# Who multiplies the spread values: VectorE or GpSimd, in the lead-in of a two-layer graph convolution

## What the reference computes

```python
def _ngcf_conv(x, W1, W2, src, dst, n_nodes):
    ones = jnp.ones(src.shape[0], dtype=x.dtype)
    deg_out = jnp.clip(jax.ops.segment_sum(ones, src, num_segments=n_nodes), 1.0)
    deg_in = jnp.clip(jax.ops.segment_sum(ones, dst, num_segments=n_nodes), 1.0)
    norm = jax.lax.rsqrt(deg_out[src] * deg_in[dst])
    h_src, h_dst = x[src], x[dst]
    msg = (h_src @ W1 + h_src * h_dst @ W2) * norm[:, None]
    return x @ W1 + jax.ops.segment_sum(msg, dst, num_segments=n_nodes)
h = jax.nn.relu(_ngcf_conv(x, W1_1, W2_1, src, dst, n))
h = _ngcf_conv(h, W1_2, W2_2, src, dst, n)
out = _layernorm(x + h)
```

## Time and profile before

| | us |
|---|---|
| median of 3 runs | 1270.73 (1262.32 to 1270.86) |
| the profiled execution | 1268.42, of it 1266.8 from the first to the last instruction |
| PE busy | 806.7 |
| DVE busy | 1003.4 |
| ACT busy | 715.0 |
| POOL busy | 810.5 |

### The profile page before, as it was taken

One profiled execution on the slowest core, in us unless ns is written; L12 is line 12 of the kernel. 1 busy time (PEld: TensorE's weight loads), 2 busy tenths in 40 slices (PEclk: granted clock), 3 DMA queues, 4 the chain that ended last, 5 costly groups with the idle time before them and its releaser, 6 DMA issues. The chain is left out here.

```text
span 1266.8 us, 33156 instructions
## 1 busy us (share of the span) xinstructions
PE 806.7 (64%) x12938; PEld 743.5 (59%) x12938; DVE 1003.4 (79%) x2582; ACT 715.0 (56%) x2723; POOL 810.5 (64%) x819
## 2 busy tenths in 40 slices
PE   1655367676767677766773566666766666766664
PEld 1554256566666666655662566666666665766664
DVE  8998578888898889888962678778878877788774
ACT  3000046665666566666662266667677667667665
POOL 6000677777777777777734777777777777667600
PEclk9999989988988898899885786888778788887885
DMA  6976112222222222222212133333333333333322
GB/s 130 199 220 280 42 37 52 53 52 52 52 52 52 53 52 52 57 51 58 53 40 58 27 68 68 77 76 76 69 69 76 77 77 77 67 67 80 67 45 48
DMA packets 148617, 93.63 MB, mean 74 GB/s; under 512 B 115880, under 2 KB 128616, under 8 KB 147948
## 3 DMA queue, kind: packets, MB, share of 16 engines
q1 hardware_dynamic: 122872, 64.77, 19.2%
q0 software_dynamic: 25472, 26.34, 12.0%
q10 hardware_dynamic: 116, 0.40, 0.1%
HBM read 52.75 MB, written 38.69 MB: 72 GB/s over the span
## 5 line engine op out<-in xcount | busy, mean ns | idle before, releaser
L591 POOL DMA_INDIRECT c_rows<-table,k_row_i x796 | 789.7, 992 | 395.7 <-issue 237.6
L608 PE MATMUL c_sum<-c_rest,c_sel 128*128 128x64 bf16 x3110 | 388.4, 215 | 0.0
L608 PE MATMUL c_sum<-c_lo,c_sel 128*128 128x64 bf16 x3110 | 388.2, 215 | 0.1
L608 PE MATMUL c_sum<-c_rows,c_sel 128*128 128x64 bf16 x1555 | 213.6, 224 | 201.5 <-DVE c_lo L746 181.9
L608 PEld LDWEIGHTS c_sum<-c_lo,c_sel 128*128 128x128 bf16 x3110 | 337.2, 113 | 0.2 <-issue 0.2
L608 PEld LDWEIGHTS c_sum<-c_rest,c_sel 128*128 128x128 bf16 x3110 | 336.6, 113 | 0.1
L608 PEld LDWEIGHTS c_sum<-c_rows,c_sel 128*128 128x128 bf16 x1555 | 180.2, 119 | 214.1 <-issue 214.1
L608 PE MATMUL c_sum<-c_yr,c_sel 128*128 128x64 bf16 x1555 | 174.1, 206 | 145.7 <-DVE c_lo L746 133.1
L608 PEld LDWEIGHTS c_sum<-c_yr,c_sel 128*128 128x128 bf16 x1555 | 156.9, 107 | 161.8 <-issue 161.8
L731 DVE TENSOR_SCALAR c_sel<-k_place,k_grid 128x512 bf16<-128x512 f16 (+2 forms) x796 | 234.8, 366 | 0.0
L660 ACT ACTIVATE c_sum<-c_sum,k_xh 128x64 f32<-128x64 f32 x784 | 172.1, 348 | 72.2 <-DVE c_sum L762 72.2
(11 more groups left out here) (134 smaller groups left out, 1074.8 us busy)
## 6 DMA issues: line engine op xcount, KB each, us to landing
c_rows<-table,k_row_i POOLq DMA_INDIRECT x796
table<-c_y SPq DMA_DIRECT2D x48, 256.0 KB
c_res<-in_x SPq DMA_DIRECT2D x48, 256.0 KB, 2.9
out<-c_y SPq DMA_DIRECT2D x48, 256.0 KB, 2.6
table<-k_xh SPq DMA_DIRECT2D x2, 3640.0 KB, 10.7
table<-k_xh SPq DMA_DIRECT2D x1, 3542.5 KB, 12.9
table<-k_xh SPq DMA_DIRECT2D x1, 1040.0 KB, 7.0
table<-k_xh SPq DMA_DIRECT2D x1, 520.0 KB, 5.5
```

Source lines behind the costliest of these rows:

```text
L591: nc.gpsimd.indirect_dma_start(out=rows[:, b % RING, i], out_offset=None, in_=tables[l], in_offset=bass.IndirectOffsetOnAxis(ap=k.row_i[:, ...
L608: last = nc.tensor.matmul(p_sum[g % BANKS][:, t - GROUP[g][0], :], sel[:, b % 2, i, n * P:(n + 1) * P], part, start=first and q == 0, stop ...
```

## The change

Frame 0 stays on VectorE. For frames 1 to 8 the four products of `spread` are issued by GpSimd, from the same operands. VectorE makes the two one-hots of a frame one frame earlier than before, so `near_s` and `near_n` have two buffers each. A new semaphore, `near_made`, tells GpSimd that they are there; before it writes, GpSimd also waits until the last piece of frame f-2 is placed. VectorE waits, before it writes a `near` buffer again, until GpSimd has used it (`spread_made`, f-1). TensorE's waits and all of VectorE's other work stay as they were.

```diff
-        near_s, near_n = sb("near_s", [P, WIN, EB * FRAME_PS[0]], F16), sb("near_n", [P, WIN, EB * FRAME_PS[0]], F16)
+        near_s, near_n = ([sb(f"{n}{j}", [P, WIN, EB * FRAME_PS[0]], F16) for j in range(2)] for n in ("near_s", "near_n"))
...
+        def spread_out(engine, f):
+            w = FRAME_PS[f]
+            shape = [P, WIN, EB, w]
+            for a in range(4):
+                last = engine.tensor_tensor(blocks(spread[f % 2][:, a], w), blocks((near_s, near_n)[a == 3][f % 2], w),
+                                            by_raw(value_t[a], f).unsqueeze(1).to_broadcast(shape), ALU.mult)
+            last.then_inc(spread_made, 1)
...
+            pool.wait_ge(copied, 5)
+            for f in range(1, FRAMES):
+                pool.wait_ge(near_made, f + 1)
+                pool.wait_ge(spread_made, f)
+                if f >= 2:
+                    pool.wait_ge(piece_placed, LAST_PIECE[f - 2] + 1)
+                spread_out(nc.gpsimd, f)
...
-            def spreads(f):
-                w = FRAME_PS[f]
+            def nears(f):
+                w, j = FRAME_PS[f], f % 2
...
-                if f:
-                    dve.wait_ge(spread_made, f)
-                V.tensor_tensor(wide(near_s), rel, win_s[:, FRAME_SHIFT[f]:FRAME_SHIFT[f] + WIN, 0:w].unsqueeze(2).to_broadcast(shape), ALU.is_equal)
-                step(V.tensor_tensor(wide(near_n), rel, win_n[:, :, 0:w].unsqueeze(2).to_broadcast(shape), ALU.is_equal))
                 if f >= 2:
-                    dve.wait_ge(piece_placed, LAST_PIECE[f - 2] + 1)
-                for a in range(4):
-                    last = V.tensor_tensor(wide(spread[f % 2][:, a]), wide((near_s, near_n)[a == 3]), by_raw(value_t[a], f).unsqueeze(1).to_broadcast(shape), ALU.mult)
-                last.then_inc(spread_made, 1)
+                    dve.wait_ge(spread_made, f - 1)
+                V.tensor_tensor(blocks(near_s[j], w), rel, win_s[:, FRAME_SHIFT[f]:FRAME_SHIFT[f] + WIN, 0:w].unsqueeze(2).to_broadcast(shape), ALU.is_equal)
+                V.tensor_tensor(blocks(near_n[j], w), rel, win_n[:, :, 0:w].unsqueeze(2).to_broadcast(shape), ALU.is_equal).then_inc(near_made, 1)
...
-            spreads(0)
+            nears(0)
+            dve.wait_ge(near_made, 1)
+            spread_out(V, 0)
+            nears(1)
             hots(1)
             for f in range(1, 6):
-                spreads(f)
+                nears(f + 1)
                 hots(2 * f)
                 add(f - 1)
                 hots(2 * f + 1)
...
-            spreads(6)
+            nears(7)
             hots(12)
             add(5)
             hots(13)
-            spreads(7)
+            nears(8)
             degrees(2)
             hots(14)
             norms(2)
             add(6)
-            spreads(8)
             hots(15)
```

More of the change, by code:

```diff
@@ L121, in prepare @@
             "ints_made", "halves_made", "turned", "copied", "rel_made", "checked"))
+        near_made = sem("near_made")
         hots_made, spread_made, piece_placed, added = sem("hots_made"), sem("spread_made"), sem("piece_placed"), sem("added")
@@ L139, in by_raw, with blocks @@
             return a[:, :].rearrange("q (b p) -> q b p", b=EB)[:, b0:b0 + n, FRAME_P0[f]:FRAME_P0[f + 1]]
+        def blocks(a, w):
+            return a[:, :, 0:EB * w].rearrange("q w (b p) -> q w b p", b=EB)
+        def spread_out(engine, f):
[5 more added lines that the diff above has]
+            last.then_inc(spread_made, 1)
         def frame(f):
@@ L371, in hots @@
                                 by_raw(lane_t, f, b0, nb).unsqueeze(1).to_broadcast([P, P, nb, w]), ALU.is_equal).then_inc(hots_made, 1)
-            def spreads(f):
-                w = FRAME_PS[f]
+            def nears(f):
+                w, j = FRAME_PS[f], f % 2
                 shape = [P, WIN, EB, w]
-                wide = lambda a: a[:, :, 0:EB * w].rearrange("q w (b p) -> q w b p", b=EB)
                 rel = by_raw(rel_t, f).unsqueeze(1).to_broadcast(shape)
-                if f:
-                    dve.wait_ge(spread_made, f)
-                V.tensor_tensor(wide(near_s), rel, win_s[:, FRAME_SHIFT[f]:FRAME_SHIFT[f] + WIN, 0:w].unsqueeze(2).to_broadcast(shape), ALU.is_equal)
-                step(V.tensor_tensor(wide(near_n), rel, win_n[:, :, 0:w].unsqueeze(2).to_broadcast(shape), ALU.is_equal))
                 if f >= 2:
-                    dve.wait_ge(piece_placed, LAST_PIECE[f - 2] + 1)
-                for a in range(4):
-                    last = V.tensor_tensor(wide(spread[f % 2][:, a]), wide((near_s, near_n)[a == 3]), by_raw(value_t[a], f).unsqueeze(1).to_broadcast(shape), ALU.mult)
-                last.then_inc(spread_made, 1)
+                    dve.wait_ge(spread_made, f - 1)
+                V.tensor_tensor(blocks(near_s[j], w), rel, win_s[:, FRAME_SHIFT[f]:FRAME_SHIFT[f] + WIN, 0:w].unsqueeze(2).to_broadcast(shape), ALU.is_equal)
+                V.tensor_tensor(blocks(near_n[j], w), rel, win_n[:, :, 0:w].unsqueeze(2).to_broadcast(shape), ALU.is_equal).then_inc(near_made, 1)
             def add(f):
```

## The result

The changed kernel took 1283.41 us (median of 4 runs, 1279.98 to 1285.21) against 1269.96 us for the kernel before: a ratio of 1.0117, 95% interval 1.008 to 1.0153. It is slower by 1.2%. The forecast was 1290, range 1265 to 1312. The profiled execution took 1282.32 us, span 1280.7.

What follows compares the result with a forecast made beforehand. The prediction took VectorE's queue in the lead-in's frames as the bound. Removing 13.2 us, adding 39.6 of GpSimd products, less 6.0 beside other work, gave +20.4 us: 1290 us, range 1265 to 1312.

Steps and rivals of the forecast that it cites:

- What bounds the kernel: In the lead-in's frames VectorE sets the pace, busy 80.27 of 82.29 us; the 1137.50 us behind move along whole.
- What is removed, 13.2 us: VectorE's queue in frames 1 to 8 loses the products and the wait between one-hots and products: 13.2 us.
- What is added: 32 products on GpSimd at 2.09 ns an element, 1.64 us for a wide one: 39.6 us.
- rival (c): GpSimd products are slower, by row cost or per element, or turns come late: 1303 to 1331 us; chance 0.20.
- The hold: In the frames, VectorE work with two SBUF inputs and GpSimd work reading SBUF run one after the other, f16 included.
- rival (a): In the frames, f16 operations on VectorE and GpSimd do not hold each other up: 1256 us; chance 0.11.
- rival (b): The hold lasts only part of each GpSimd product, 16.6 us in all: 1266 to 1268 us; chance 0.12.
- The turns: In a wide frame GpSimd's four products alternate with VectorE's two `near`s and two `hot`s; waits for `spread` and buffers cost nothing.
- the case of late turns: GpSimd gets a turn only when VectorE idles, `spread` comes late, TensorE work is exposed: up to 18 us more, 1308.
- The sum: For the whole kernel, -13.2 + 39.6 - 6.0 = +20.4 us, giving 1290 us, 1.5% slower.
- the price of a turn: In the frames, VectorE is held for each GpSimd product, except 6.0 of the 39.6 us beside other work.
- the 6.0 of the prediction: GpSimd time beside VectorE work without a second SBUF input: adds 3.5 us, reciprocals of three norms 2.5 us.

Runs made afterwards that it cites:

- Run 2: The changed kernel with `hot` reading `lane_t` from its PSUM bank, so with one SBUF input: 1256.97 us against 1265.69 for the kernel before, ratio 0.9929.
- the control: The kernel before, products on VectorE, with only the edit that makes `hot` read `lane_t` from PSUM: ratio 0.9997.
- Runs 4 to 6: The kernel before plus 32 unread GpSimd operations: two-input products, iotas that read nothing, one-input multiplications, in turn; last norm later by 26.6, 0.04 and 10.2 us.
- run 8: The changed kernel with three `near` buffers instead of two: ratio 1.0082 to the kernel before on the second chip.
- run 7: The changed kernel's order, but only product 3 of frames 1 to 8 on GpSimd, products 0 to 2 on VectorE: ratio 1.0017 to the kernel before.
- run 3: The kernel before with `hot` reading `lane_t` from PSUM and the frames' banks moved, products still on VectorE: ratio 0.9997, interval 0.9965 to 1.0029.
- run 5: The kernel before plus 32 GpSimd iotas of the products' sizes into a tile nobody reads, on the second chip: 1702.40 us, run once, against 1705.16.

## Why the prediction was right, and where its sizes were off

**What bounds the kernel.** Right. The frames' VectorE queue moved, and all of the difference came from there; the layers moved by 2.1 us of 1137.

**What is removed, 13.2 us.** Run 2 confirms it. The last norm came 11.1 us earlier than before; 0.9 of that is the control's own gain, and 2.8 us of holds are still in it, on the wide one-hots (4.9 + 4.7 in busy time, against 3.4 + 3.4). 11.1 - 0.9 + 2.8 = 13.0.

**What is added.** A wide product was priced at 1.64 us and took 1.53; the narrow ones at 0.94, 0.47 and 0.29 and took 1.02, 0.59 and 0.38. The sum, 39.6, was 38.6. The row cost of rival (c), 23 ns for each of 56 rows, is not there.

**The hold.** Right, and this was the choice that decided the sign. The records with 4-byte inputs carried over to f16 (rival (a) falls), and held VectorE for about a product's length, 1.4 us (rival (b), 0.7 us, falls). Runs 4 to 6 show that it takes reading on GpSimd's side, and run 2 that for `hot`, a TENSOR_TENSOR, it takes the second SBUF input on VectorE's side. This is the rule of the Trainium skill, "SBUF — State Buffer", section "Who interferes with whom"; this case's trace now agrees for f16 as well, 1.92 us for a one-hot of 0.56.

**The turns.** Wrong in detail. The prediction said that GpSimd finishes its four products in four turns and that VectorE's new wait and TensorE's for `spread` stay free. In frame 1 the first product, issued at 38.49, got no turn before the add at 46.83, VectorE then idled 4.4 us, and once more 5.3 us behind TensorE. VectorE was busy for 0.89 of the frames instead of the 0.98 of before, where the prediction had it near full, and only two wide `hot` pieces grew by a whole turn. This is the case of late turns that stood under rival (c), with TensorE waiting for `spread` as (c) said. It hardly added to the sum: in the idle 9.7 us GpSimd ran product after product, which it would otherwise have run against held work, and run 8 shows such an exchange. The prediction did not argue this. It had all that VectorE pays as holds, and a third of it came as idle time; that the total stayed near is in this part luck.

**The sum.** The forecast of 20.4 us is 5.5 above the 14.9 of the last norm. 1.0 of it is the products' own length. The other 4.5 is the term that was mis-sized, the price of a turn: GpSimd's time that VectorE did not pay stood at 6.0 us and was 10.5. The trace tells where the 10.5 lay, by an estimate that places each product at the last 1.53 us of its record (1.02, 0.59 or 0.38 for a narrow one), since the records hold the wait as well. 5.9 us lay beside adds (2.8), reciprocals (2.5) and degrees (0.6): that is the 6.0 of the prediction, rightly priced. 10.1 us lay in VectorE's idle time or in the short gaps between its steps. 22.6 us lay beside instructions that were held, and these were held 18.1 us in all. So VectorE did not pay a product's full length for each turn: `near_n` grew by 1.44 and 1.36 us for a product of 1.53, and the one-hots of 128x112 by 0.40 for one of 0.59. Why a turn costs less than the product was not tested. The rest of the difference, 1.0 us, is the layers' and the store's (+1.0 and -2.1).

## What to carry to other kernels

Before a piece of VectorE's work goes to GpSimd, look at what VectorE does meanwhile: a GpSimd instruction that reads SBUF and a VectorE TENSOR_TENSOR with two SBUF inputs ran one after the other here, in f16 as in 4-byte types, and then the work costs VectorE nearly GpSimd's duration (1.4 of 1.53 us) in place of its own (0.48). It was free beside a TENSOR_TENSOR that takes one of its inputs from PSUM, so the change to try first is to leave an operand in the bank where TensorE put it: that turned +1.2% into -0.7%. And an idle stretch in front of a wait is no gain in waiting: where the two engines take turns, removing the wait moved 4.4 us of it elsewhere and took 0.2 us off the end.

## What the runs showed of the hardware that was not expected

- The first product of the changed kernel, issued at 38.49 during a `hot`, got no turn when VectorE went on to `near_s` (42.07), `near_n` and the next `hot` (43.03), which all ran at their own length; it ran beside the add. The same stands in run 8, and in run 7 for its one product past the next `hot` at 44.46, both on the second chip. The two-input shadow, issued at 37.65 during a `hot`, did get its turn at the next change (`near_s` at 41.19, 1.92 us), and so did most products of later frames. What decides the turn stays open.
- A VectorE TENSOR_SCALAR of 128x109 f32, its one input in SBUF, was held as well, beside a product with the change (first row) and not without one before (second row). The RECIPROCAL of 128x109 at 86.75, also with one SBUF input, kept its 0.83 us beside a product. So one input is not always safe; what tells the two apart was not tested.

```profile
90.09 1.50 DVE L422 TENSOR_SCALAR a_square<-a_square 128x109 f32<-128x109 f32 x1
```

```profile
76.11 0.22 DVE L409 TENSOR_SCALAR a_square<-a_square 128x109 f32<-128x109 f32 x1
```

- In the control of run 3 the narrow `hot` of 128x2048 took 1.22 us with `lane_t` from PSUM, 1.87 with it from SBUF; the wide ones took 3.88 either way.
- The two chips gave the kernel before 1265.69 and 1705.16 us. The lead-in was the same to 0.1 us (last norm at 123.20 in run 5, 123.16 in the earlier trace rows); the layers were not. The mean granted TensorE clock of the whole run was 0.865 in the changed kernel's profile and 0.72 in run 5's. Why the chips differ was not looked into.
